# Local-attention stack on one core: pairs of 512-column instructions written as one of 1024, banks renumbered

## The chip, the cores and the metric

One NeuronCore of a Trainium2 chip (trn2) runs the whole program. The metric is the device time of one execution in microseconds, from the first to the last instruction of the core. TensorE does the matmuls and transposes; VectorE and ScalarE work between SBUF and PSUM (128 partitions, 8 banks of 512 float32 columns); GpSimd works in SBUF; SyncE issues the DMAs.

## What is computed

The input is 16 sequences of 128 tokens and 128 features. One cross-attention over a context of the same size comes first, then six layers, each of local attention (16 heads of 64, windows of 32 tokens that also see the window before) and a gated feed-forward. All of it is float32; the big products are made of three products of rounded parts.

```python
def attn_layer(x, Wqkv, qs, ksc, Wo):
    qkv = x @ Wqkv                      # 128 -> 3 * 1024
    q, k, v = jnp.split(qkv, 3, -1)     # 16 heads of 64 each
    q = l2norm(q) * qs
    k = l2norm(k) * ksc
    q = q * cos * scale + rotate_half(q) * sin * scale
    k = k * cos / scale + rotate_half(k) * sin / scale
    sim = q @ k.T * 8                   # window i against windows i - 1 and i
    attn = softmax(where(mask, -inf, sim))
    return (attn @ v) @ Wo

def ffn_layer(x, g, bln, W1, b1, W2, b2):
    xn = (x - mu) / sqrt(var + 1e-05) * g + bln
    a, gate = jnp.split(xn @ W1 + b1, 2, -1)
    return a * gelu(gate) @ W2 + b2

x = x + tanh(g_xattn) * cross_attention(layernorm(x), ctx)
h = layernorm(x)
for l in range(6):
    h = h + attn_layer(shift_tokens(h), ...)
    h = h + ffn_layer(h, ...)
out = x + tanh(g_ffn) * h
```

## The kernel before

The sequences go in pairs: 6 layers x 8 pairs are 48 pairs, and each of the pair's two items, r = 0 and r = 1, has 128 tokens on the partitions. After the cross-attention (the first 60 us) every engine runs one loop over 50 turns, in which pair `it` begins (lag 0), pair `it - 1` is in its attention (lag 1) and pair `it - 2` in its out-projection and feed-forward (lag 2). The order of the steps within a turn is written out by hand for each engine, and each engine works strictly in that order; semaphores hold it until its inputs are there. `on(lag)` says whether the pair with this lag exists.

Of one item, the work goes as follows. TensorE makes four chunks of 512 columns of q and k (`chunk`, L1199) and two of v (`v_chunk`, L1203). ScalarE squares each chunk (`square`, L623), VectorE sums the squares per head (`squares`) and multiplies the chunk by the rotation's tables (`straight`, `swapped`), GpSimd adds these (`add`) and normalises (`normalise`). TensorE transposes q and k (`turn_qk(s)`, L1207, for half s = 0 or 1 of the heads, into the two banks of `turn_qk` 2s and 2s + 1), and ScalarE copies these four banks out one by one (`heads_out(k)`, L647). ScalarE puts the mask into two score banks (`masks`), TensorE adds the scores (`scores`), VectorE takes maxima and subtracts them (`maxima(e)` L926, `minus_maxima(e)` L932, one bank e each), ScalarE takes exponentials (`exp(e)` L661), VectorE sums (`row_sums(e)` L939, then one `reciprocals`), GpSimd divides (`divide(e)` L460). TensorE transposes the probabilities (`turn_p`, L1235), ScalarE copies them (`p_out(g)` L667), TensorE multiplies by the values (`values`), ScalarE copies the output (`o_out(h)` L674). v is copied out of its banks by ScalarE (`v_out(j)` L655), and SyncE moves parts of it to other partitions by DMA (`shifted_values`).

Of a pair, the rest is: `project_out` on TensorE, `residual` on VectorE (L951), `centre` and `variance` on TensorE with `deviations` (L684) and `inverse_deviation` (L690, an Ln at L695 and an Exp at L698) on ScalarE, `normal` (L959) on VectorE, `upper_x` (L700) on ScalarE, `lower_x` (L967) on VectorE, the up-projection `up(1)`, `up(0)`, `up(2)` (L1292), `gelu` on ScalarE, `gated` (L975) on VectorE, `down` on TensorE and `feed_back` (L988) on VectorE.

Banks are shared: `BANK_USERS` lists for each bank its users in a turn, as (kind, number, r, lag), in the order of use. Before TensorE (or `masks`) writes a bank, `freed` makes it wait for the instruction that empties it of its last user (`bank_left`). Three such neighbourhoods matter below. `turn_qk(1, 1, 0)` (the transposes of half 1, lag 1, r = 0) writes the bank that `turn_qk(0, 1, 0)` had, and so waits for `heads_out(0, 1, 0)`. `v_chunk(1, 0, 0)` writes the bank of scores(1), r = 1, and waits for `minus_maxima(1, 1, 1)`. `turn_qk(0, 1, 0)` writes the bank of `v_chunk(1, 0, 0)` and waits for `v_out(1, 0, 0)`; `chunk(2, 0, 0)` follows `turn_qk(1, ...)`'s second bank of r = 1, emptied by `heads_out(1, 1, 1)`.

## Time and profile before

| | |
|---|---|
| median of 3 runs | 1455.85 us (1452.92 to 1457.2) |
| the profiled execution | 1451.59 us, span 1449.7 us |
| TensorE busy | 1357.1 us, 94% of the span |
| VectorE busy | 1294.6 us, 89% |
| ScalarE busy | 1266.6 us, 87% |
| GpSimd busy | 1184.0 us, 82% |
| matmuls / VectorE / ScalarE / GpSimd instructions | 30176 / 2400 / 2523 / 1162 |

The page's tenths over the span show the same picture from slice 4 to slice 38: all engines at 8 or 9 tenths, one turn like the other. So the reader should look at one turn with its times, and at the waits. In the page PE is TensorE, DVE VectorE, ACT ScalarE, POOL GpSimd; L12 is line 12 of the kernel. In a timeline, "x2" is two instructions of one kind in a row; their time is from the start of the first to the end of the last. Ends of matmuls are modelled.

### The profile page before, as it was taken

How to read it: one execution, taken by the hardware profiler on the slowest of the kernel's cores; microseconds unless marked ns; L12 is line 12 of the kernel's file. 1: busy time of each engine (PE TensorE's matmuls, PEld its weight loads, DVE VectorE, ACT ScalarE, POOL GpSimd, SP SyncE). 2: the span in 40 equal slices, each digit the busy share in tenths (PEclk: the TensorE clock that was granted, in tenths of full speed). 3: DMA queues.
4: the chain of work that ended last, by engine and by line, in shares of the span. 5: the costliest groups of instructions: out<-in, count | busy, mean ns of one | idle time of the engine just before them, and what ended most of it. 6: DMA issues, size and time to landing. Idle time of an engine off the chain costs nothing.

```text
span 1449.7 us, 76627 instructions
## 1 busy us (share of the span) xinstructions
PE 1357.1 (94%) x30176; PEld 1094.5 (75%) x30176; DVE 1294.6 (89%) x2400; ACT 1266.6 (87%) x2523; POOL 1184.0 (82%) x1162
## 2 busy tenths in 40 slices
PE   6589999999999999999999999999999999999985
PEld 4467777877777777777777777777777778777774
DVE  6688999999999999999999999999999999999973
ACT  6578999999999999999999999999999999899873
POOL 2687888888888888888888888888888888888860
PEclk9899999999999999999999999999999999999998
DMA  5221112131111222111122111113111112111111
GB/s 148 81 57 41 38 48 57 36 89 42 51 39 47 57 57 68 42 50 39 47 70 61 50 43 50 39 46 95 36 43 36 36 37 77 43 29 43 43 31 30
DMA packets 61752, 75.09 MB, mean 52 GB/s; under 512 B 8462, under 2 KB 35340, under 8 KB 61708
## 3 DMA queue, kind: packets, MB, share of 16 engines
q1 hardware_dynamic: 61708, 74.51, 18.8%
q8 instruction: 27, 0.44, 0.1%
q14 instruction: 17, 0.14, 0.0%
HBM read 18.90 MB, written 1.05 MB: 14 GB/s over the span
## 4 chain that ended last, share of the span: by engine, by line
PE 47%; DVE 19%; issue 15%; ACT 6%; POOL 5%; DVEq 2%; ACTq 0%; POOLq 0%
PE bank L1275 12%; PE bank L1178 6%; PE bank L1266 6%; DVE ss L906 5%; PE bank L1191 5%; PE bank L1179 4%; PE bank L1180 4%; DVE psum L943 4%; POOL u L444 3%; DVE u L913 3%; PE bank L1228 3%; PE bank L1311 3%; DVE t L922 3%; PE bank L1300 2%; ACT gate L714 2%
## 5 line engine op out<-in xcount | busy, mean ns | idle before, releaser
L444 POOL TENSOR_TENSOR u<-u,t 128x512 f32<-128x512 f32 x384 | 490.5, 1283 | 84.3 <-DVE t L922 68.5
L457 POOL TENSOR_TENSOR u<-u,rn 128x512 f32<-128x512 f32 x384 | 388.9, 1045 | 0.0
L628 ACT ACTIVATE sq<-bank 128x512 f32<-128x512 f32 x384 | 234.0, 610 | 64.0 <-PE bank L1180 62.0
L1178 PE MATMUL bank<-Wl,xsh 128*128 (+1 forms) x576 | 268.0, 465 | 15.4 <-POOL xsl L439 11.3
L463 POOL TENSOR_TENSOR P<-P,rs 128x512 f32<-128x512 f32 x192 | 196.6, 1045 | 95.0 <-DVE rs L948 95.0
L922 DVE TENSOR_TENSOR t<-bank,TS 128x512 f32<-128x512 f32 x384 | 258.7, 684 | 6.1 <-ACT sq L628 2.1
L906 DVE TENSOR_REDUCE ss<-sq 128x8 f32<-128x512 f32 x384 | 255.6, 676 | 6.4 <-issue 6.4
L913 DVE TENSOR_TENSOR u<-bank,TC 128x512 f32<-128x512 f32 x384 | 255.1, 675 | 1.3 <-ACT sq L628 1.3
L652 ACT COPY qkT<-bank 128x512 f32<-128x512 f32 x384 | 225.2, 603 | 13.5 <-PE bank L1191 6.4
L1179 PE MATMUL bank<-Wh,xsl 128*128 (+1 forms) x576 | 228.8, 397 | 0.0
L1180 PE MATMUL bank<-Wh,xsh 128*128 (+1 forms) x576 | 228.7, 397 | 0.0
L1275 PE MATMUL bank<-OT,WoS 128*128 128x256 f32 x768 | 176.7, 384 | 1.2 <-issue 1.2
L1191 PEld LDWEIGHTS bank<-shape_constants,u 64*128 64x128 f32 x3072 | 112.9, 140 | 85.4 <-issue 85.4
L1275 PEld LDWEIGHTS bank<-OT,WoS 128*128 128x128 f32 x768 | 147.9, 193 | 23.8 <-issue 1.5
L1266 PE MATMUL bank<-PT,v 64*64 64x64 f32 (+1 forms) x3072 | 154.9, 227 | 3.9 <-ACT PT L671 2.7
L1266 PEld LDWEIGHTS bank<-PT,v 64*64 64x64 f32 x3072 | 132.6, 135 | 29.2 <-issue 22.9
L1266 PE MATMUL bank<-PT,vs 64*64 64x32 f32 (+1 forms) x6144 | 153.7, 217 | 0.0
L1178 PEld LDWEIGHTS bank<-Wl,xsh 128*128 128x128 f32 x576 | 109.0, 189 | 57.7 <-issue 17.7
L1191 PE MATMUL bank<-shape_constants,u 64*128 64x64 f32 x3072 | 137.9, 230 | 14.0 <-issue 10.4
L929 DVE TENSOR_REDUCE nm<-bank 128x8 f32<-128x512 f32 x192 | 123.3, 684 | 29.6 <-PE bank L1228 29.6
L1228 PE MATMUL bank<-qkT 64*32 64x64 f32 (+1 forms) x12288 | 140.1, 220 | 8.5 <-issue 7.2
L1228 PEld LDWEIGHTS bank<-qkT 64*32 64x32 f32 x12288 | 123.7, 105 | 29.0 <-issue 27.0
(92 smaller groups left out, 2732.1 us busy)
## 6 DMA issues: line engine op xcount, KB each, us to landing
vs<-v SPq DMA_DIRECT2D x384, 128.0 KB, 2.3
Wraw<-in_L_ffn_Wqkv_dram SPq DMA_DIRECT2D x72, 117.5 KB, 2.1
WoS<-in_L_ffn_Wo_dram SPq DMA_DIRECT2D x6, 512.0 KB, 4.0
W1h<-Wh SPq DMA_DIRECT2D x6, 341.0 KB, 2.6
W1l<-Wl SPq DMA_DIRECT2D x6, 341.0 KB, 2.9
Wraw<-in_L_ffn_W_dram SPq DMA_DIRECT2D x12, 116.0 KB, 2.2
out_dram<-X SPq DMA_DIRECT2D x4, 256.0 KB, 2.7
W2S<-in_L_ffn_W_dram SPq DMA_DIRECT2D x6, 128.0 KB
```

The source lines that it names most:

```text
L444: nc.gpsimd.tensor_tensor(u[:, r, c], u[:, r, c], t2[:, r, c % 2], ALU.add).then_inc(add_done[c], 1)
L457: nc.gpsimd.tensor_tensor(by_head(u[:, r, c]), by_head(u[:, r, c]), spread(rn[:, r, HC * c:HC * c + HC], HC, DH), ALU.mult).then_inc(qk_re ...
L906: nc.vector.tensor_reduce(ss[:, r, HC * c:HC * c + HC], by_head(square_out(c, r)), AX, ALU.add).then_inc(ss_done[c], 1)
L913: nc.vector.tensor_tensor(by_head(u[:, r, c]), by_head(bank_of("chunk", c, r)[:]), TC[:, layer(it - lag), c % 2].broadcast_to([128, HC, DH ...
L922: nc.vector.tensor_tensor(halves(t2[:, r, c % 2]), halves(bank_of("chunk", c, r)[:])[:, :, ::-1, :], TS[:, layer(it - lag), c % 2].broadca ...
L1178: nc.tensor.matmul(out, x[0], Wl[:, w], start=True, stop=False)
L1179: nc.tensor.matmul(out, x[1], Wh[:, w], start=False, stop=False)
L1180: nc.tensor.matmul(out, x[0], Wh[:, w], start=False, stop=True).then_inc(done, 1)
L1191: i = nc.tensor.transpose(bank_of(kind, k + g, r)[:, at:at + 64], src[p, 128 * t:128 * t + 128], ident[p, 64 * g:64 * g + 64])
L1228: i = nc.tensor.matmul(bank_of("scores", e, r)[64 * w2 + 32 * a:64 * w2 + 32 * a + 32, at:at + (32 if w == 0 else 64)], qkT[f, r, s, 0, t, ...
L1266: i = nc.tensor.matmul(to, keys, prob, start=True, stop=True)
L1275: i = nc.tensor.matmul(bank_of("Wo")[:, 0:2 * S], WoS[:, k], OT[:, k].rearrange("p r s -> p (r s)"), start=(k == 0), stop=(k == INNER // 1 ...
```

## The change

Pairs of instructions that do the same to the two banks or halves of one item become one instruction over 1024 columns:

- VectorE: `maxima`, `minus_maxima`, `row_sums`, for both r (12 instructions a turn become 6).
- ScalarE: `exp` and `v_out` for both r, `heads_out(0)` and `heads_out(1)` for both r (`all_heads_out(0)`), `p_out(0)` and `p_out(1)` for r = 0 (`all_p_out`). `heads_out(2)`, `heads_out(3)` and the `p_out` of r = 1 stay two.
- GpSimd: `divide` for both r.

So that two banks can be one operand, the eight banks become one tensor and are renumbered; the users of each bank and their order stay. For five pairs the first bank has the higher number, and the two are then read in falling order (`[:, ::-1]`). The semaphores of the two halves become one; those of the head and probability copies get a set for each r.

The joined instruction stands where one of the two stood. `all_heads_out(0, 1, 0)` takes the place of `heads_out(0, 1, 0)`, ahead of a square; `all_heads_out(0, 1, 1)` that of `heads_out(1, 1, 1)`, ahead of `inverse_deviation`; `v_out(1, 1)` that of `v_out(0, 1, 1)`, ahead of a square and the masks of r = 1; `row_sums(1, 0)` that of `row_sums(1, 1, 0)`, behind `squares(1, 0, 0)`.

```diff
-        K = [bank(str(k)) for k in range(8)]
+        PS = es.enter_context(nc.psum_tensor("banks", [128, 8, 512], F32))
+        K = [PS[:, k] for k in range(8)]
...
+        def banks_of(kind, k=0, r=0):
+            b, b2 = (bank_place(kind, k + e, r)[0] for e in range(2))
+            return PS[:, b:b + 2] if b < b2 else PS[:, b2:b + 1][:, ::-1]
...
-                    divide(0, 2, 0)
-                    divide(1, 2, 0)
+                    divide(2, 0)
...
+                def all_heads_out(s, lag, r):
+                    pair = it - lag
+                    act.wait_ge(qk_turned[s], n_(pair * 2 + r) + 1)
+                    act.wait_ge(sc_full[s], n_(pair * 2 + r) - 1)
+                    nc.scalar.copy(qkT[:, r, s].rearrange("p w t (g i) -> p g (w t) i", g=2),
+                                   banks_of("turn_qk", 2 * s, r).rearrange("p g (k i) -> p g k i", i=64)
+                                   ).then_inc(qk_out[r][2 * s], 1)
...
                 if on(1):
-                    heads_out(0, 1, 0)
+                    all_heads_out(0, 1, 0)
                     square(1, 1, 1)
-                    heads_out(1, 1, 0)
                     heads_out(2, 1, 0)
...
-                    v_out(0, 1, 1)
+                    v_out(1, 1)
...
                     masks(0, 1, 1)
-                    v_out(1, 1, 1)
-                    exp(1, 1, 0)
-                    exp(0, 1, 0)
+                    exp(1, 0)
...
                     heads_out(3, 1, 1)
-                    heads_out(1, 1, 1)
+                    all_heads_out(0, 1, 1)
                 if on(2):
                     inverse_deviation(2)
-                if on(1):
-                    heads_out(0, 1, 1)
...
-                    p_out(1, 1, 0)
-                    p_out(0, 1, 0)
+                    all_p_out(1, 0)
...
-                    exp(0, 1, 1)
-                    exp(1, 1, 1)
+                    exp(1, 1)
                     o_out(1, 1, 0)
                 if on(0):
-                    v_out(1, 0, 0)
-                    v_out(0, 0, 0)
+                    v_out(0, 0)
...
+                def maxima(lag, r):
+                    n = (it - lag) * 2 + r
                     dve.wait_ge(scores_full[r], n_(n) + 1)
+                    nc.vector.tensor_reduce(nm[:, r], heads_of_two(banks_of("scores", 0, r)), AX, ALU.max).then_inc(mx_done, 1)
...
-                    row_sums(0, 1, 0)
                 if on(0):
                     squares(1, 0, 0)
                 if on(1):
-                    row_sums(1, 1, 0)
+                    row_sums(1, 0)
                     reciprocals(1, 0)
...
-                    maxima(0, 1, 1)
-                    maxima(1, 1, 1)
-                    minus_maxima(1, 1, 1)
-                    minus_maxima(0, 1, 1)
+                    maxima(1, 1)
+                    minus_maxima(1, 1)
```

## Rows read from the trace of the kernel before

**Rows 1.** Stretches: length, busy us of PE, PEld, DVE, ACT, POOL, clock, DMA.
```profile
662.00:944.00 282.00, 273.39 (x6243) 221.34 (x6242) 262.64 (x471) 258.63 (x511) 246.04 (x241) 1.00 0.19 51
```

**Rows 2.** Waits of whole span: who for whom, us in total, times, longest.
```profile
DVE R L956 <- PE bank L1275: 46.1, 48, 12.9
...
DVE hT L982 <- ACT gate L714: 25.3, 47, 1.7
...
PE bank L1300 <- DVE xfl L972: 18.1, 46, 1.2
...
PE bank L1191 <- issue: 10.4, 46, 0.3
```

**Rows 3.** Groups of instructions by shape: count | busy us, mean ns | idle before.
```profile
L444 POOL TENSOR_TENSOR u<-u,t 128x512 f32<-128x512 f32 x384 | 490.5, 1283 | 84.3 <-DVE t L922 68.5 <-DVE u L913 10.9
...
L628 ACT ACTIVATE sq<-bank 128x512 f32<-128x512 f32 x384 | 234.0, 610 | 64.0 <-PE bank L1180 62.0 <-DVE ss L906 1.7
...
L463 POOL TENSOR_TENSOR P<-P,rs 128x512 f32<-128x512 f32 x192 | 196.6, 1045 | 95.0 <-DVE rs L948 95.0
...
L936 DVE TENSOR_TENSOR P<-bank,nm 128x512 f32<-128x512 f32 x192 | 123.2, 684 | 1.7
...
L956 DVE TENSOR_TENSOR R<-bank,R 64x256 f32 x90 | 38.1, 423 | 31.0 <-PE bank L1275 30.4
...
L439 POOL TENSOR_TENSOR xsl<-R,xsh 128x256 fp32r<-128x256 f32 x48 | 32.8, 683 | 20.6 <-ACT xsh L621 14.3 <-issue 6.3
...
L688 ACT ACTIVATE sqx<-bank 128x256 f32<-128x256 f32 x48 | 18.2, 380 | 7.7 <-PE bank L1283 7.7
```

**Rows 4.** Timeline, ScalarE, one turn: start, us, line, operation, count [idle before].
```profile
699.98 0.60 ACT L628 ACTIVATE sq<-bank 128x512 f32<-128x512 f32 x1 [0.50 <-PE bank L1180]
...
703.84 0.42 ACT L698 ACTIVATE rstdx<-lvx 128x256 f32<-128x256 f32 x1
...
706.63 1.08 ACT L671 COPY PT<-bank 128x512 f32<-128x512 f32 x2 [0.20 <-PE bank L1191]
...
710.06 1.20 ACT L714 ACTIVATE gate<-bank,feature_columns 128x256 f32<-128x256 f32 x3
```

**Rows 5.** Timeline, VectorE, the same turn and the next one's start.
```profile
699.60 0.86 DVE L956 TENSOR_TENSOR R<-bank,R 64x256 f32 x2 [0.68 <-PE bank L1275]
...
704.66 0.49 DVE L964 SCALAR_TENSOR_TENSOR bank<-bank,feature_columns,rstdx 128x256 f32<-128x256 f32 x1
...
706.25 0.47 DVE L972 SCALAR_TENSOR_TENSOR xfl<-bank,feature_columns,xfh 128x256 fp32r<-128x256 f32 x1
...
709.74 1.29 DVE L936 TENSOR_TENSOR P<-bank,nm 128x512 f32<-128x512 f32 x2
711.54 1.27 DVE L982 SCALAR_TENSOR_TENSOR hT<-bank,feature_columns,gate 128x256 f32<-128x256 f32 x3 [0.51 <-ACT gate L714]
...
727.77 0.86 DVE L956 TENSOR_TENSOR R<-bank,R 64x256 f32 x2 [0.69 <-PE bank L1275]
```

**Rows 6.** Timeline, TensorE, the same turn.
```profile
705.88 0.71 PE L1191 MATMUL bank<-shape_constants,P 64*128 64x64 f32 x16
706.97 0.32 PE L1300 MATMUL bank<-xfh,W1l 128*85 128x256 f32 x1 [0.38 <-DVE xfl L972]
...
710.86 0.39 PE L1178 MATMUL bank<-Wl,xsh 128*128 x1
```

**Rows 7.** Timeline, all engines, 713.5 to 718.6.
```profile
714.09 1.08 ACT L659 COPY v<-bank 128x512 f32<-128x512 f32 x2
...
715.14 0.72 PE L1191 MATMUL bank<-shape_constants,u 64*128 64x64 f32 x16
...
715.34 0.97 DVE L994 SCALAR_TENSOR_TENSOR R<-bank,feature_columns,R 64x256 f32 x2
...
716.00 0.63 ACT L652 COPY qkT<-bank 128x512 f32<-128x512 f32 x1
...
716.97 0.71 PE L1191 MATMUL bank<-shape_constants,u 64*128 64x64 f32 x16 [0.22 <-issue]
```

More of the change, by code:

```diff
@@ L261, in bank_left, with when_left, both_left, item @@
                 other, ok, orr, lag = users[at]
-                before = pair + users[place][3] + turns - lag
-                if not isinstance(pair, int) or 0 <= before < PAIRS:
-                    if other in OF_PAIR:
-                        return [(s, n_(before + (LAYER_PAIRS if s is h_ready else 0)) + 1) for s in FREED[other](ok, orr)]
-                    return [(s, n_(before * 2 + orr) + 1) for s in FREED[other](ok, orr)]
-            return []
+                away = users[place][3] + turns - lag
+                if not isinstance(pair, int) or 0 <= pair + away < PAIRS:
+                    return [(s, other in COUNTS_PAIRS, orr, away) for s in FREED[other](ok, orr)]
+            return []
+        def when_left(pair, users):
+            for s, per_pair, r, away in users:
+                if per_pair:
+                    yield s, n_(pair + away + (LAYER_PAIRS if s is h_ready else 0)) + 1
+                else:
+                    yield s, n_((pair + away) * 2 + r) + 1
+        def bank_left(pair, kind, k=0, r=0):
+            return when_left(pair, user_before(pair, kind, k, r))
+        def both_left(pair, kind, k, r):
+            first, second = user_before(pair, kind, k, r), user_before(pair, kind, k + 1, r)
+            return when_left(pair, first + [user for user in second if user not in first])
         def column(at, pair, per=1, k=0, rows=slice(0, 128)):
             return fc[rows, ds(pair // LAYER_PAIRS * per + (at + k), 1)]
+        def item(t, r):
+            if len(t.shape) == 5:
+                return t[:, r].rearrange("p e g c -> p (e g) c")
+            return t[:, r].rearrange("p e g -> p (e g)")
         def layer(pair):
@@ new lines, in v_out, with exp @@
+                def v_out(lag, r):
+                    n = (it - lag) * 2 + r
+                    act.wait_ge(v_all_full[r], n_(n) + 1)
+                    act.wait_ge(pv_full, n_(n) - 1)
+                    nc.scalar.copy(v[:, r].rearrange("p (j n) -> p j n", j=2), banks_of("v", 0, r)).then_inc(v_ready, 1)
+                def exp(lag, r):
+                    n = (it - lag) * 2 + r
+                    act.wait_ge(sc_out, n_(n) + 1)
+                    ps = P[:, r].rearrange("p e g c -> p (e g c)")
+                    nc.scalar.activation(ps, ps, ACT.Exp).then_inc(exp_done, 1)
@@ L674, in o_out, with all_p_out @@
+                def all_p_out(lag, r):
+                    pair = it - lag
+                    act.wait_ge(P_turned, n_(pair * 2 + r) + 1)
+                    act.wait_ge(pv_full, n_(pair * 2 + r) - 1)
+                    nc.scalar.copy(PT[:, r].rearrange("p e (t g i) -> p g (e t) i", g=2, i=64),
+                                   banks_of("turn_p", 0, r).rearrange("p g (k i) -> p g k i", i=64)
+                                   ).then_inc(PT_ready[r][0], 1)
                 def o_out(h, lag, r):
@@ L1003, in step @@
                     straight(2, 1, 1)
-                    maxima(0, 1, 0)
-                    maxima(1, 1, 0)
-                    minus_maxima(0, 1, 0)
-                    minus_maxima(1, 1, 0)
+                    maxima(1, 0)
+                    minus_maxima(1, 0)
                 if on(0):
```

160 lines of the change are left out of this document (73 added, 87 removed).

## The prediction, made before the changed kernel was built or run

> **What bounds the kernel now.** I read the table of stretches first. In the middle of the span TensorE is busy for 273.39 of 282 us, VectorE for 262.64, ScalarE for 258.63 and GpSimd for 246.04, and the granted clock is 1.00 of its upper level, 2.4 GHz [rows 1]. So TensorE is nearest to the bound, and its idle time there is 8.6 us of 282, or 0.86 us for each turn of the loop. A turn is 28.17 us: the residual of one turn starts at 699.60, that of the next at 727.77 [rows 5]. The turns repeat almost exactly, so one of them can be walked through. No join touches a matmul. The change can therefore give back at most those 0.86 us a turn, and it takes time wherever TensorE has to wait longer.
>
> The list of waits then says where the 0.86 us lie [rows 2]: TensorE waits for the low half of the normalised features (`lower_x`, L972) 46 times, 18.1 us in all, 0.39 us each; and ahead of transposes (L1191) 46 times, 10.4 us, put down to "issue", 0.23 us each. The second has no releaser in the view, so I looked at the timeline of all engines [rows 7]. The transposes are those of `turn_qk(1,1,0)` at 716.97. They need the bank that `heads_out(0,1,0)` empties, and this copy runs 716.00 to 716.63. From ScalarE's end to TensorE's start are 0.34 us. That is the whole wait. VectorE's waits for the out-projection (46.1 us) and for the gate (25.3 us) [rows 2] show that it is paced by others.
>
> So the path that closes a turn is: end of the out-projection, residual, VectorE's and ScalarE's layernorm chain, `lower_x`, then TensorE nearly without a gap from 706.97 [rows 6] to the end of the next out-projection, with the transposes at 716.97 the one gap in which it waits for ScalarE.
>
> **What a joined instruction costs.** On ScalarE the square of 512 columns takes 610 ns and that of 256 takes 380 [rows 3]: 256 columns are 0.23 us, 512 are 0.46. A joined copy is so at most 0.61 + 0.46 = 1.07 us. Two copies one behind the other take 1.08 us in all [rows 4], as each starts before the last has quite ended. A join there saves 0.01 to 0.03 us at the end of the pair; I take 0.02. On VectorE, 512 columns of a tensor_tensor out of a bank take 684 ns and 256 take 423 (on 64 partitions, the nearest row) [rows 3], so 512 more are 0.52 us and a joined one 1.21 against 1.29 for the pair at 709.74 [rows 5]: 0.08 saved. On GpSimd a `divide` of 512 takes 1045 ns; the nearest operation in two sizes takes 1283 for 512 and 683 for 256 [rows 3], so 512 more columns would be 1.20 of 1.28 and 0.08 us are saved by a join. The two divides are between 2.09 and 2.01 us, and off the path either way. None of these rows shows 1024 columns over two banks, nor banks read in falling order, which the new layout needs for five of its pairs. I take it at the slope above; an end at nothing extra and an end at 0.1 us each bound it.
>
> Per turn VectorE loses 6 instructions, ScalarE 7, GpSimd 2. That is 6 x 0.08 = 0.5 us of VectorE and 7 x 0.02 = 0.14 us of ScalarE. Most of it lies where these engines wait for TensorE anyway (0.50 us before the square at 699.98 [rows 4], 0.68 before the residual at 699.60 [rows 5]), and is worth nothing.
>
> The rows say that ScalarE's second copy costs 0.47 us on top of the first's 0.61, and 0.46 of that are columns. The Trainium skill, "VectorE: DVE Perf Modes", section on the TRN2 errata, gives ScalarE 172 cycles plus one a column for a bank source and says that one large tile pays the fixed part once. By an estimate from that page seven joins would free 1.0 us of ScalarE a turn, and 512 more columns would cost 0.43 us and not 0.46, so that the sum below would end at 1496 and not 1498. Where instructions are back to back, the rows don't bear the larger saving out.
>
> **What it delays.** A joined instruction hands over its first half only when both are done. I went through every pair and asked who waits for the first half, and how long before that one's start it was ready.
>
> 1. *The head copies before the inverse deviation.* `heads_out(1,1,1)` stood before `inverse_deviation`, `heads_out(0,1,1)` behind it. Now both come first. Its second instruction, the Exp at 703.84, ends at 704.26 [rows 4] and comes 0.46 later: 704.72. From ScalarE's end to VectorE's start take 0.28 (the last gate ends at 711.26 [rows 4], hT starts at 711.54 [rows 5]). So `normal` starts at 705.00 and not 704.66 [rows 5]: 0.34. VectorE itself is late too: `squares(1,0,0)` now stands directly behind the residual (699.60 + 0.86 = 700.46) and its square ends at 700.58 [rows 4]; with the same hand-over it starts at 700.86, 0.40 us idle, less 0.08 for the joined sums: 704.98. The two run side by side, the later one counts. I take 0.30 (0.25 to 0.34), and `lower_x` and the up-projection at 706.97 [rows 6] move by as much.
> 2. *The score differences.* `v_chunk(1,0,0)` at 710.86 [rows 6] needs the bank of scores(1,1,1). `minus_maxima(1)` came first of its pair and was done at 709.74 + 0.68 = 710.42; VectorE to TensorE takes 0.25 (`lower_x` ends at 706.72 [rows 5], TensorE starts at 706.97 [rows 6]), so the bank was ready 0.19 before it was wanted. Joined, it is ready 0.52 later, less 0.08 for the joined maxima. 0.52 - 0.08 - 0.19 = 0.25. VectorE and TensorE both carry delay 1, which cancels.
> 3. *The first head copy of r = 0.* `turn_qk(1,1,0)` waits for `heads_out(0,1,0)`, now `all_heads_out`, 0.46 longer. Its start can be 0.10 nearer to its transposes: they end at 715.86 and the copy starts at 716.00 [rows 7], while elsewhere it takes 0.04 (706.59 [rows 6] to 706.63 [rows 4]). 0.46 - 0.10 = 0.36. TensorE already waits here, so all of it shows. Behind it TensorE has `turn_p`, the last v chunks, values, scores and `chunk(3,0,0)`; ScalarE's next copies need these transposes, so its chain to `x_parts` and the xsl moves along, and nothing catches up.
>
> Other joins hold back a first half and hide it. `v_out(0,0)` gives its first bank at 715.1 + 0.34, where `turn_qk(0,1,0)` stands at 715.14 [rows 7]; but delays 1 and 2 have moved that to 715.7, so it is covered as long as they are there, and costs 0.3 if they are not. The joined `all_heads_out(0,1,1)` frees chunk(2,0,0)'s bank 0.46 later, which eats TensorE's idle time before the up-projection, not more. The joined exp and sums of r = 1 make the reciprocals 0.5 late; `divide` and `turn_p` follow them with under 0.4 us to spare after delay 3. The joined v copies of r = 1 bring exp(1,0) forward by 0.3, to no one's use. SP's shifted values waited for the second v copy before as well. The bank numbers alone cost nothing; they name the same sequence of users.
>
> **The sum.** 0.30 + 0.25 + 0.36 = 0.91 us a turn. The three occur in 46, 47 and 47 turns: 13.8 + 11.8 + 16.9 = 42.5 us. The profiled execution took 1451.59 us (span 1449.7), so its successor would take 1494; the median of the runs is 4.3 us above the profiled one, which gives 1498.
>
> **The rivals.** *Hidden in part*: one or two of the delays are covered by slack I misjudge. Delays 1 and 2 rest on 0.2 us of slack each; delay 3 alone gives 17 us, 1473, and two of them 1482. For it: hand-over times are read from one place each. *Faster*: TensorE's wait at 716.97 is not for the copy but for something else ahead of it in the same queues (`feed_back`, which ends at 716.31 [rows 7], is the other one in question), and the chain to `lower_x` has the slack. Then ScalarE and VectorE reach their points 0.1 to 0.2 us earlier a turn, 0.2 x 46 = 9 us, 1447. It decides where the fixed part of an instruction is above 0.2 us; the pairs show under 0.1, and the end-to-start 0.34 of ScalarE recurs, so I give it little. The Trainium skill's fixed costs ("VectorE: DVE Perf Modes", the same section) would point this way. *No effect*: joins split again or all within slack, 1456. *More*: reading over two banks costs 0.1 us extra each and falls on three delays and the v copies, 0.3 to 0.4 us a turn more, 1515.
>
> **Chances.** Forecast 0.60 (own range 1484 to 1506); hidden in part 0.17; more 0.07; faster 0.10; no effect 0.06. Differences under 0.3% (4 us) can't be told from none. So faster 0.10, same 0.06, slower 0.84. The range takes the first two and half of "more": 1462 to 1514.
>
> **What the profile of the changed kernel would show.** A turn of 29.1 us; TensorE's busy share in the middle down from 97% to 94%; its wait before `turn_qk(1,1,0)` at about 0.6 us; a new wait of 0.25 us before `v_chunk(1,0,0)` released by VectorE's P; joined copies of 1.05 us on ScalarE and 1.21 on VectorE. Joined ones under 0.9 us would make me wrong, as would turns in which `turn_qk(1,1,0)` doesn't follow the end of the joined copy by 0.34 us.

## The result, and the profile after

The changed kernel takes 1485.01 us, the median of 4 runs (1481.63 to 1487.11), beside 1454.38 us for the kernel before in 4 runs (1448.48 to 1457.2). The ratio is 1.0214, with a 95% interval of 1.0175 to 1.0252: slower by 30.6 us, where the forecast was slower by 42.5. The profiled execution of the changed kernel took 1481.63 us, with a span of 1479.8.

The page's first part: busy time of each engine, its share of the span, instructions.

```profile
PE 1374.1 (93%) x30176; PEld 1100.9 (74%) x30176; DVE 1286.0 (87%) x2112; ACT 1244.8 (84%) x2187; POOL 1171.9 (79%) x1066
```

Every engine but TensorE has less to do than before (VectorE 1294.6, ScalarE 1266.6, GpSimd 1184.0), and the kernel is slower all the same. The middle of the span, as in [rows 1]:

```profile
662.00:944.00 282.00, 270.43 (x5992) 217.31 (x5986) 253.77 (x400) 247.89 (x432) 237.59 (x216) 1.00 0.18 50
```

TensorE is idle for 11.6 us of 282 and not 8.6. A turn is 28.92 us, so that is 1.19 us a turn and not 0.86. This is less than half of what a turn has grown by. The rest, 0.42 us a turn, is counted as busy, 27.73 us and not 27.31 for the same matmuls: a product is recorded at 0.39 to 0.40 us while the one behind it can start 0.23 after it, so the first 0.17 us or so of a wait behind a product disappears in its modelled end. So I take waits from starts and not from idle time. The granted clock is 1.00 here as before. The waits of the whole span, as in [rows 2] (us in total, times, longest):

```profile
DVE banks L991 <- ACT rstdx L734: 22.3, 48, 3.2
...
PE banks L1211 <- ACT qkT L679: 21.3, 46, 0.5
PE banks L1320 <- DVE xfl L999: 20.8, 47, 1.2
...
DVE psum L971 <- ACT P L693: 12.7, 47, 0.5
```

The wait before `turn_qk(1,1,0)`, 10.4 us in [rows 2] and put down to "issue", is now 21.3 us and names the joined head copy. The forecast's new wait ahead of `v_chunk(1,0,0)` isn't in this list; its 0.18 us are among those that count as busy, and show in the starts of TensorE's rows below. The joined instructions by shape (count, busy us, mean ns, idle before), as in [rows 3]:

```profile
L486 POOL TENSOR_TENSOR P<-P,rs 128x1024 f32<-128x1024 f32 x96 | 183.0, 1906 | 111.6 <-DVE rs L976 111.6
...
L963 DVE TENSOR_TENSOR P<-banks,nm 128x1024 f32<-128x1024 f32 x96 | 117.6, 1225 | 7.3
...
L693 ACT ACTIVATE P<-P 128x1024 f32<-128x1024 f32 x96 | 101.8, 1061 | 4.0 <-DVE P L963 3.4
L679 ACT COPY qkT<-banks 128x1024 f32<-128x1024 f32 x96 | 98.9, 1030 | 11.4 <-PE banks L1211 11.3
L687 ACT COPY v<-banks 128x1024 f32<-128x1024 f32 x96 | 96.5, 1006 | 0.2 <-PE banks L1200 0.2
```

One turn on ScalarE, as in [rows 4] (start, us, line, operation):

```profile
712.23 1.04 ACT L679 COPY qkT<-banks 128x1024 f32<-128x1024 f32 x1
713.14 0.51 ACT L731 ACTIVATE lvx<-banks,cols 128x256 f32<-128x256 f32 x1
713.68 0.42 ACT L734 ACTIVATE rstdx<-lvx 128x256 f32<-128x256 f32 x1
...
723.83 1.02 ACT L687 COPY v<-banks 128x1024 f32<-128x1024 f32 x1
...
726.02 1.01 ACT L679 COPY qkT<-banks 128x1024 f32<-128x1024 f32 x1 [0.20 <-PE banks L1211]
```

The same turn on VectorE, as in [rows 5], from one residual to the next. The two residuals bound the turn that the table below takes apart:

```profile
709.09 0.86 DVE L983 TENSOR_TENSOR R<-banks,R 64x256 f32 x2 [0.59 <-PE banks L1295]
710.10 0.69 DVE L934 TENSOR_REDUCE ss<-sq 128x8 f32<-128x512 f32 x1 [0.16 <-ACT sq L649]
...
714.49 0.49 DVE L991 SCALAR_TENSOR_TENSOR banks<-banks,feature_columns,rstdx 128x256 f32<-128x256 f32 x1 [0.38 <-ACT rstdx L734]
...
719.51 1.23 DVE L963 TENSOR_TENSOR P<-banks,nm 128x1024 f32<-128x1024 f32 x1
...
738.00 0.86 DVE L983 TENSOR_TENSOR R<-banks,R 64x256 f32 x2 [0.60 <-PE banks L1295]
```

And on TensorE, as in [rows 6] and [rows 7]: the up-projection, `v_chunk(1,0,0)`, `turn_qk(0,1,0)`, `turn_qk(1,1,0)`.

```profile
716.81 0.32 PE L1320 MATMUL banks<-xfh,W1l 128*85 128x256 f32 x1 [0.42 <-DVE xfl L999]
...
720.57 0.28 PE L1322 MATMUL banks<-xfh,W1h 128*128 128x256 f32 x1
720.88 0.50 PE L1198 MATMUL banks<-Wl,xsh 128*128 x1
...
725.20 0.71 PE L1211 MATMUL banks<-shape_constants,u 64*128 64x64 f32 x16
...
727.27 0.71 PE L1211 MATMUL banks<-shape_constants,u 64*128 64x64 f32 x16 [0.46 <-ACT qkT L679]
```

`v_chunk(1,0,0)` starts 0.31 us after the matmul ahead of it. In the kernel before it was 0.12, and that matmul's row is not among the rows ahead:

```profile
710.74 0.29 PE L1302 MATMUL bank<-xfh,W1h 128*128 128x256 f32 x1
```

With these starts a turn can be cut into parts, and the parts of two kernels compared. The parts are, each from start to start: residual to up-projection (A), up-projection to `v_chunk(1,0,0)` (B), from there to `turn_qk(0,1,0)` (C), to `turn_qk(1,1,0)` (D), and to the next residual (E). All in us, read from the same timelines of each kernel near 700 us; where two turns in a row differ, both values stand. The last column is a turn near there; it is within 0.03 us of the median over all the turns of that profile.

| kernel | A | B | C | D | E | turn |
|---|---|---|---|---|---|---|
| before | 7.37 | 3.90 | 4.29 | 1.83 | 10.80 | 28.17 |
| after | 7.72 | 4.08 | 4.32 | 2.07 | 10.72 | 28.92 |
| all joined (control) | 7.72 | 4.07 | 4.27 | 2.19 | 10.74, 10.82 | 29.05 |
| banks only | 7.37 | 3.89 | 4.28 | 1.83 | 10.75, 10.81 | 28.15 |
| heads of r = 0 apart | 7.72 | 4.07 | 4.27 | 1.81 | 10.77, 10.85 | 28.65 |
| heads of r = 1 apart | 7.37 | 4.08 | 4.29 | 2.19 | 10.73, 10.83 | 28.70 |
| scores of r = 1 apart | 7.72 | 3.89 | 4.39 | 2.19 | 10.74, 10.83 | 28.97 |
| scores 1 and v 0 apart | 7.72 | 3.89 | 4.26 | 2.20 | 10.75, 10.84 | 28.84 |
| three apart | 7.37 | 3.88 | 4.40 | 1.76 | 10.78, 10.89 | 28.24 |
| four apart | 7.38 | 3.88 | 4.26 | 1.78 | 10.91, 10.99 | 28.24 |
| sums first | 7.72 | 4.08 | 4.26 | 2.19, 2.24 | 10.73, 10.84 | 29.07 |
| before, waits turned | 7.37 | 3.90 | 4.29 | 1.59 | 10.93, 10.96 | 28.05 |
| after, waits turned | 7.72 | 4.07 | 4.27 | 1.99 | 10.72 | 28.79 |
| six apart, waits turned | 7.37 | 3.89 | 4.29 | 1.59 | 10.85, 10.95 | 28.03 |

After against before, a turn grows by 0.35 + 0.18 + 0.03 + 0.24 - 0.08 = 0.72 us in this turn, and by 0.73 between the medians of the 47 turns (28.18 and 28.91). From the first residual to the last the profiles take 1327.1 and 1360.0 us: 32.9 more. Ahead of the first residual the changed kernel's profiled execution is 2.8 us shorter (101.8 against 104.6), with a granted clock of 0.91 against 0.87 from 60 to 100 us. Outside the loop differences of some us come and go between executions with the granted clock there (0.74 in the profile of `e3_heads1_apart`, from 60 to 100 us), so below I read turns first and medians second. The experiments were run in three sets, each with runs of the kernel before beside it (medians 1453.99, 1452.85 and 1455.10 us), so two experiments are compared by their ratios and not by their times.

### The profile page after: what moved, and what is told of

Its sections match the earlier page's. It is cut to its first block, busy times and chain, and to the rows that moved or that the text cites. A ratio compares the mean times of both kernels' runs of the same rounds, so it can differ in the third digit from the quotient of the medians.

```text
span 1479.8 us, 75430 instructions
## 1 busy us (share of the span) xinstructions
PE 1374.1 (93%) x30176; PEld 1100.9 (74%) x30176; DVE 1286.0 (87%) x2112; ACT 1244.8 (84%) x2187; POOL 1171.9 (79%) x1066
## 3 DMA queue, kind: packets, MB, share of 16 engines
HBM read 18.90 MB, written 1.05 MB: 13 GB/s over the span
## 4 chain that ended last, share of the span: by engine, by line
PE 56%; DVE 15%; issue 12%; ACT 8%; POOL 3%; DVEq 1%; ACTq 0%; POOLq 0%
PE banks L1295 11%; PE banks L1286 8%; PE banks L1198 7%; PE banks L1199 5%; PE banks L1200 5%; PE banks L1211 5%; DVE u L941 4%; PE banks L1331 4%; DVE psum L971 4%; PE banks L1320 3%; DVE ss L934 3%; ACT sq L649 3%; PE banks L1248 3%; PE banks L1321 2%; PE banks L1322 2%
## 5 line engine op out<-in xcount | busy, mean ns | idle before, releaser
L649 ACT ACTIVATE sq<-banks 128x512 f32<-128x512 f32 x384 | 231.3, 603 | 84.8 <-PE banks L1200 83.4
L1198 PE MATMUL banks<-Wl,xsh 128*128 (+1 forms) x576 | 280.5, 487 | 17.8 <-POOL xsl L462 11.6
L486 POOL TENSOR_TENSOR P<-P,rs 128x1024 f32<-128x1024 f32 x96 | 183.0, 1906 | 111.6 <-DVE rs L976 111.6
L950 DVE TENSOR_TENSOR t<-banks,TS 128x512 f32<-128x512 f32 x384 | 258.4, 683 | 4.8 <-ACT sq L649 1.6
L941 DVE TENSOR_TENSOR u<-banks,TC 128x512 f32<-128x512 f32 x384 | 254.7, 674 | 1.8 <-ACT sq L649 1.8
L1199 PE MATMUL banks<-Wh,xsl 128*128 (+1 forms) x576 | 228.8, 397 | 0.0
L1200 PE MATMUL banks<-Wh,xsh 128*128 (+1 forms) x576 | 228.3, 396 | 0.0
L1295 PE MATMUL banks<-OT,WoS 128*128 128x256 f32 x768 | 175.5, 382 | 1.2 <-issue 1.2
L1211 PE MATMUL banks<-shape_constants,u 64*128 64x64 f32 x3072 | 137.9, 229 | 26.5 <-ACT qkT L679 21.3
L1286 PE MATMUL banks<-PT,v 64*64 64x64 f32 (+1 forms) x3072 | 155.3, 228 | 2.7 <-ACT PT L706 1.4
L1286 PE MATMUL banks<-PT,vs 64*64 64x32 f32 (+1 forms) x6144 | 154.0, 217 | 0.0
```

The lines of the kernel that those rows point to most:

```text
L649: nc.scalar.activation(square_out(c, r), bank_of("chunk", c, r)[:], ACT.Square).then_inc(sq_done[c], 1)
L941: nc.vector.tensor_tensor(by_head(u[:, r, c]), by_head(bank_of("chunk", c, r)[:]), TC[:, layer(it - lag), c % 2].broadcast_to([128, HC, DH ...
L1198: nc.tensor.matmul(out, x[0], Wl[:, w], start=True, stop=False)
L1199: nc.tensor.matmul(out, x[1], Wh[:, w], start=False, stop=False)
L1200: nc.tensor.matmul(out, x[0], Wh[:, w], start=False, stop=True).then_inc(done, 1)
L1211: i = nc.tensor.transpose(bank_of(kind, k + g, r)[:, at:at + 64], src[p, 128 * t:128 * t + 128], ident[p, 64 * g:64 * g + 64])
```

## The experiments

Theory: each of the three delays of the forecast comes from one join that makes TensorE wait, and undoing that join takes that delay alone away. Rivals: joined instructions over two banks are slow in themselves; the path over VectorE's sums sets `normal`; the layout of the banks matters.

All kernels below compute everything. Most of them come from one form of the changed kernel in which any join can be undone by a switch. Where a diff below shows instructions, it shows what the switch makes of them. For this form, each half and each r has a semaphore of its own, counted by pairs:

```diff
-        mx_done, sc_out, sum_done, rs_done = (sem(s) for s in ("mx_done", "sc_out", "sum_done", "rs_done"))
+        mx_done, sc_out, sum_done, exp_done, P_ready, v_ready = (
+            [sems(name + str(r), 2) for r in range(2)] for name in ("mx_done", "sc_out", "sum_done", "exp_done", "P_ready", "v_ready"))
+        rs_done = sem("rs_done")
```

**All joined, in this form (`e0_all_joined`).** The control: nothing else is changed against the changed kernel. It was run after the next eight, whose expectations therefore start from the changed kernel's 28.92 us a turn and not from the control's 29.05.

> Control for the runs before: all joins of the changed kernel, with the semaphores of the experiments (one for each half and r, counted by pairs). In the changed kernel TensorE starts 0.24 us after the end of the joined head copy, in the experiments 0.36 to 0.39. TensorE's queue tells why, I think: there the wait for the copy stands in front of the register instruction that works out the next wait's value, together with that for the normalised heads. My theory: hand-over 0.38, a turn of 29.07 us, ratio 1.026 to 1.030, and e7 (29.08) is no slower than its control. Rival (e7's order of sums costs 0.16 itself): 28.92 us.

Ratio to before 1.0271 (1.0241 to 1.0301), 1494.27 us. A turn is 29.05 us and not 28.92, and the difference lies in D, 2.19 against 2.07; C is 0.05 shorter, and E longer by about as much. ScalarE and TensorE there:

```profile
699.71 1.02 ACT L698 COPY qkT<-banks 128x1024 f32<-128x1024 f32 x1 [0.16 <-PE banks L1297]
```

```profile
701.08 0.71 PE L1297 MATMUL banks<-shape_constants,u 64*128 64x64 f32 x16 [0.58 <-ACT qkT L698]
```

The copy ends at 700.73 and the transposes start 0.35 later. In the changed kernel they follow their copy by 727.27 - 727.03 = 0.24. The copy and the transposes are the same, only the bookkeeping of semaphores differs. So this control is what the experiments are compared with, and the 0.11 are a question of their own (the last three experiments).

**The banks alone (`e1_banks_only`).** New numbers and one tensor, every join undone:

```diff
-                    all_heads_out(0, 1, 0)
+                    heads_out(0, 1, 0)
                     square(1, 1, 1)
+                    heads_out(1, 1, 0)
...
-                    maxima(1, 1)
-                    minus_maxima(1, 1)
+                    maxima(0, 1, 1)
+                    maxima(1, 1, 1)
+                    minus_maxima(1, 1, 1)
+                    minus_maxima(0, 1, 1)
```

> The eight banks as one tensor and renumbered, every instruction in its two parts and in the order of the kernel before. My theory (three waits on a first half cost the time): ratio 1.000 to the kernel before, a turn of 28.17 us. Rival (the layout itself costs, through other banks being neighbours): a good part of the 2.1%, a turn of 28.4 us or more.

Ratio 0.9998 (0.998 to 1.0017), 1453.65 us; a turn of 28.15. The layout costs nothing that can be told from none, and the loss is in the joins. That the joined instructions cost nothing extra for two banks or for a falling order is in the rows of the changed kernel: 1006 to 1061 ns on ScalarE, where the slope of [rows 3] gives at most 1070, and 1225 on VectorE, where it gives 1210. The head copy of r = 0 reads its banks in falling order and takes 1.01 us, that of r = 1 in rising order and takes 1.04.

**The head copies of r = 0 apart (`e2_heads0_apart`).**

```diff
-                    all_heads_out(0, 1, 0)
+                    heads_out(0, 1, 0)
                     square(1, 1, 1)
+                    heads_out(1, 1, 0)
```

> The changed kernel with the head copy of r = 0 in two again, at the old places. My theory: the transposes turn_qk(1,1,0) wait for half a copy, the 0.24 us between the two transposes come back, 46 times: 11 us less than the changed kernel, 1474 us, ratio 1.0135. The size that I forecast (0.36) would give 17 us less. Rival (joined instructions are slow of themselves or load a shared port): 1 or 2 us, as one of twelve joins is gone.

Ratio 1.0149 (1.0109 to 1.0189), 1476.13 us. A turn is 28.65, 0.40 under the control (0.37 by the medians of all turns); D falls from 2.19 to 1.81, and nothing else moves by more than 0.01. This is delay 3, alone, at the control's hand-over. The expectation had 0.24, the changed kernel's size.

**The head copies of r = 1 apart (`e3_heads1_apart`).**

```diff
-                    all_heads_out(0, 1, 1)
+                    heads_out(1, 1, 1)
                 if on(2):
                     inverse_deviation(2)
+                if on(1):
+                    heads_out(0, 1, 1)
```

> The changed kernel with the head copy of r = 1 in two again, the second half behind the inverse deviation. My theory: the Exp of the inverse deviation ends 0.35 us sooner, normal and lower_x follow: up to 0.35 us a turn, 16 us less, 1469 us, ratio 1.010. If the joined sums behind squares(1,0,0) hold VectorE too, as I wrote beforehand, only about 0.05 us come back and the ratio stays at 1.020.

Ratio 1.0156 (1.0118 to 1.0193), 1476.96 us. A turn is 28.70, 0.35 under the control, all of it in A (7.72 to 7.37). This is delay 1, alone. This join delays a second thing, the bank of `chunk(2,0,0)`, which starts 4.33 us after the residual in the changed kernel and 4.11 in the kernel before. That isn't what sets A: TensorE still has 0.42 us idle before the up-projection, and waits there for `lower_x`.

**The score maxima and differences of r = 1 apart (`e4_scores1_apart`).**

```diff
-                    maxima(1, 1)
-                    minus_maxima(1, 1)
+                    maxima(0, 1, 1)
+                    maxima(1, 1, 1)
+                    minus_maxima(1, 1, 1)
+                    minus_maxima(0, 1, 1)
```

> The changed kernel with maxima and differences of r = 1 in two again. v_chunk(1,0,0) then starts 0.18 us sooner in the turn. Each delay by itself: 8 us less, ratio 1.016. My theory with the cover I named: the joined v copy of r = 0 ends 0.35 us before turn_qk(0,1,0) starts and holds it, so that TensorE loses there what it gained: within 2 us of the changed kernel, ratio 1.020.

Ratio 1.027 (1.0232 to 1.0307), 1493.54 us: no gain that the times show against the control's 1494.27. The turns say why. B falls from 4.07 to 3.89, so delay 2 is 0.18 and it is gone, but C rises from 4.27 to 4.39. ScalarE's and TensorE's rows there:

```profile
705.21 1.02 ACT L712 COPY v<-banks 128x1024 f32<-128x1024 f32 x1
```

```profile
705.36 0.57 PE L1284 MATMUL banks<-Wl,xsh 128*128 x1
706.46 0.71 PE L1297 MATMUL banks<-shape_constants,u 64*128 64x64 f32 x16
```

The joined v copy ends at 706.23, and `turn_qk(0,1,0)`, which needs its bank, starts at 706.46, 1.10 after the product ahead of it. Without a wait it is 0.97 (below). The v copy is ready to take the place of delay 2. C takes back 0.12 of the 0.18; the 0.06 that should be left are 3 us, and the medians don't show them.

**The same with the v copies of r = 0 apart (`e9_scores1_v0_apart`).** To test that reading:

```diff
-                    v_out(0, 0)
+                    v_half_out(1, 0, 0)
+                    v_half_out(0, 0, 0)
```

> The changed kernel with two joins in two again: scores of r = 1 and v copy of r = 0. The scores alone gave nothing back (28.96 against 28.92 us a turn), which I put down to the v copy: it would hold turn_qk(0,1,0) as soon as TensorE gets there sooner. If so, both together give 0.15 to 0.2 us: 28.75 us a turn. If the scores' join costs nothing at all: 28.9.

Ratio 1.0253 (1.0225 to 1.028), 1486.72 us. A turn is 28.84, 0.13 under the last one and 0.21 under the control. The interval overlaps those of the last experiment and of the control, so the times alone don't tell these three apart; their turns do. C is back at 4.26:

```profile
698.59 1.08 ACT L706 COPY v<-banks 128x512 f32<-128x512 f32 x2
```

```profile
698.74 0.57 PE L1284 MATMUL banks<-Wl,xsh 128*128 x1
699.71 0.72 PE L1297 MATMUL banks<-shape_constants,u 64*128 64x64 f32 x16
```

The product is now followed by the transposes after 0.97, with the copies starting at the same place of the turn (0.15 ahead of that product in both kernels). The v copy was the cover.

**The row sums ahead of the squares' sums (`e7_sums_first`).** The rival for delay 1: VectorE itself is late at `normal` because `squares(1,0,0)` stands directly behind the residual and waits.

```diff
+                if on(1):
+                    row_sums(1, 0)
                 if on(0):
                     squares(1, 0, 0)
                 if on(1):
-                    row_sums(1, 0)
                     reciprocals(1, 0)
```

> The changed kernel with the joined sums of r = 0 ahead of squares(1,0,0) and not behind it. This tells what delays normal: VectorE's own queue (0.16 us idle before squares(1,0,0)) or the Exp on ScalarE. By the profile of the changed kernel normal waits 0.38 us for the Exp, so the order on VectorE is worth nothing: a turn of 28.92 us, ratio 1.021. If it were VectorE's queue: 28.8 us.

Ratio 1.0304 (1.0281 to 1.0328), 1496.77 us; a turn of 29.07 beside 29.05. VectorE's row for `normal`:

```profile
722.71 0.49 DVE L1066 SCALAR_TENSOR_TENSOR banks<-banks,feature_columns,rstdx 128x256 f32<-128x256 f32 x1 [0.63 <-ACT rstdx L765]
```

VectorE now has 0.63 us to spare ahead of it, where it had 0.38 in the changed kernel, and `normal` still starts 5.41 us after the residual (5.40 in the changed kernel). ScalarE's Exp sets it, and not VectorE.

**Three apart (`e5_three_apart`).** The edits of `e2_heads0_apart`, `e3_heads1_apart` and `e4_scores1_apart` together. In the common form each group of joins is a pair of switches, for r = 0 and r = 1:

```diff
-HEADS = [True, True]
+HEADS = [False, False]
...
-SCORES = [True, True]
+SCORES = [True, False]
```

> The changed kernel with the three named joins in two again: head copies of r = 0 and r = 1, scores of r = 1. If nothing but them cost time, the turn is that of the kernel before, 28.17 us, or less. By the cover I named, the joined v copy of r = 0 now holds turn_qk(0,1,0) by about 0.2 us and the head copy behind it by 0.1 to 0.15: a turn of 28.3 us, ratio 1.004.

Ratio 1.0046 (1.0029 to 1.0063), 1459.93 us. A turn is 28.24, 0.81 under the control. Three joins make nearly the whole loss; 0.07 a turn is left, with C at 4.40 held by the v copy as above.

**Four apart (`e6_four_apart`).** The v copies of r = 0 apart as well, as in `e9_scores1_v0_apart`:

```diff
-VS = [True, True]
+VS = [False, True]
```

> As the last, and the v copy of r = 0 in two as well. The joins that are left (maxima and differences of r = 0, both sums, both exponentials, v copy of r = 1, probability copy of r = 0, both divides) have no one waiting for a first half. My theory: a turn of 28.10 to 28.17 us, ratio 0.996 to 1.001. Rival (joined instructions cost of themselves): at least half of the 0.75 us a turn is still there, 28.5 us.

Ratio 1.0017 (1.0002 to 1.0031), 1455.94 us, and yet the turn is 28.24 again. C falls to 4.26 as it should, and E rises by as much, from 10.78 to 10.91. TensorE and GpSimd at `turn_qk(1,1,0)` and `turn_p`:

```profile
690.55 0.72 PE L1297 MATMUL banks<-shape_constants,u 64*128 64x64 f32 x16 [0.18 <-issue]
691.16 0.71 PE L1297 MATMUL banks<-shape_constants,P 64*128 64x64 f32 x16
```

```profile
688.91 1.91 POOL L500 TENSOR_TENSOR P<-P,rs 128x1024 f32<-128x1024 f32 x1 [1.37 <-DVE rs L1051]
```

The divide ends at 690.82, and `turn_p` starts 0.34 later, 0.61 after `turn_qk`; where the divide is early, it starts 0.52 after it. So 0.09 of the 0.13 are the chain of exp, sums, reciprocals and divide, the next limit. The other 0.04 weren't traced. The expectation of 28.10 to 28.17 us was missed for this reason.

**The kernel before, its two waits turned (`e13_before_waits_turned`).** Now for the 0.11 us by which the changed kernel's hand-over beats that of its own control. The traces hold the instructions of TensorE's queue too, which are not counted as busy (`PEldq`; line, operation, ns, start). Ahead of `turn_qk(1,1,0)` the kernel before has an instruction that waits for the head copy, a register instruction that waits for the normalised heads, and one that waits for `feed_back` and adds to a counter:

```profile
L1173 PEldq EVENT_SEMAPHORE  x1: 51/51/51, 716.7 to 716.7; - x1
L1173 PEldq ALU_OP  x1: 32/32/32, 716.8 to 716.8; - x1
L1186 PEldq EVENT_SEMAPHORE  x1: 51/51/51, 716.9 to 716.9; - x1
```

In the changed kernel the register instruction is the one that waits for the copy, and only the last one stands behind it:

```profile
L1205 PEldq ALU_OP  x1: 32/32/32, 727.1 to 727.1; - x1
L1206 PEldq EVENT_SEMAPHORE  x1: 51/51/51, 727.2 to 727.2; - x1
```

With the trace's finer times, the copy of the kernel before ends at 716.63, the three start at 716.66, 716.77 and 716.86, the first weights load at 716.94 and the first transpose starts at 716.97. In the changed kernel the copy ends at 727.03, the two start at 727.07 and 727.16, the weights at 727.24, the transpose at 727.27. The control has three again, as the kernel before. In the built program the count that the changed kernel's wait for the copy needs is worked out just ahead of it, by a register instruction that waits for the heads; in the control the v copies are counted by pairs too, so that this count is there already, and the wait for the copy comes first again.

The wait for the copy is the one that is met last. Theory: what stands behind it in the queue is worked off after the copy's end, and so is paid every turn. Put it last, and the hand-over is shorter. Rival: 0.34 us is a fixed time from ScalarE to TensorE, and the 0.24 has another cause. The edit is the order of two lines in `turn`, and so for all transposes:

```diff
-                    freed(lag, kind, k, r)
                     freed(lag, kind, k + 1, r)
+                    freed(lag, kind, k, r)
```

> The kernel before, with one edit: ahead of transposes TensorE waits for the second bank's last user first and for the first bank's last user last, so that the wait for the head copy stands on the transpose itself and the register work for the other wait is done before. No join. If register work behind a wait is part of the hand-over, the 0.34 us from the copy to turn_qk(1,1,0) fall by 0.10 to 0.15: a turn of 28.03 us, ratio 0.996. If the hand-over is the semaphore's own time: no change, 28.17.

Ratio 0.9958 (0.9943 to 0.9973), 1448.78 us: faster than the kernel before by 0.4%. The wait for the copy now stands in the last instruction of the queue, together with that for `feed_back`. This instruction, ScalarE, TensorE and GpSimd:

```profile
L1186 PEldq EVENT_SEMAPHORE  x1: 325/325/325, 686.6 to 686.6; - x1
```

```profile
686.27 0.63 ACT L652 COPY qkT<-bank 128x512 f32<-128x512 f32 x1
```

```profile
687.00 0.71 PE L1191 MATMUL bank<-shape_constants,u 64*128 64x64 f32 x16
687.60 0.72 PE L1191 MATMUL bank<-shape_constants,P 64*128 64x64 f32 x16
```

```profile
685.22 2.05 POOL L463 TENSOR_TENSOR P<-P,rs 128x512 f32<-128x512 f32 x2 [1.09 <-DVE rs L948]
```

The copy ends at 686.90, the waiting instruction at 686.94, and TensorE starts at 687.00: 0.10 and not 0.34, so D is 0.24 shorter, and A, B and C are as before. E gives 0.13 to 0.16 back, of which, as in `e6_four_apart`, the divide explains a part: the divides end at 687.27, and `turn_p` starts 0.33 later and 0.60 after `turn_qk`, not 0.52. So the 0.34 is no fixed time from ScalarE to TensorE. 0.12 us a turn are left, times 47 makes 5.6, and the medians differ by 6.3.

**The changed kernel, its two waits turned (`e14_after_waits_turned`).**

```diff
-            return when_left(pair, first + [user for user in second if user not in first])
+            return when_left(pair, second + [user for user in first if user not in second])
```

> The changed kernel with the same edit. Its hand-over is 0.24 us; with the wait on the transpose itself 0.05 to 0.10 less: a turn of 28.84 us, ratio 1.018. If the hand-over has nothing to do with register work: 28.92, ratio 1.021.

Ratio 1.016 (1.013 to 1.019), 1480.14 us. The last instruction of the queue now waits for the copy, and alone:

```profile
L1206 PEldq EVENT_SEMAPHORE  x1: 51/51/51, 731.9 to 731.9; - x1
```

The hand-over is 0.15 us where it was 0.24; the turn goes from 28.92 to 28.79. The interval overlaps that of the changed kernel (1.0175 to 1.0252), so here too it is the turns that tell. The same lever works in both kernels. C falls from 4.32 to 4.27 as well.

**Six apart and the waits turned (`e15_six_apart_waits_turned`).** What is left of the change when every join that was found to hold TensorE is undone, the exponentials and sums of r = 1 among them, so that its divide is early:

```diff
-VS = [True, True]
-EXPS = [True, True]
+VS = [False, True]
+EXPS = [True, False]
...
-SUMS = [True, True]
+SUMS = [True, False]
```

with the three edits of `e5_three_apart` and that of `e14_after_waits_turned`.

> The joins that no one waits on, with the turned waits: maxima and differences, exponentials and sums of r = 0 joined, v copy of r = 1, probability copy of r = 0, divides; the head copies, the scores, exponentials and sums of r = 1 and the v copy of r = 0 in two. In e6 turn_p waited 0.08 us for the divided P of r = 1; with exponentials and sums in two it shouldn't. My theory: as e13, 28.0 us a turn, ratio 0.995; joins are worth nothing beyond it. If joins that hold back no one gave time to the path: below 27.9 us.

Ratio 0.995 (0.9934 to 0.9966), 1449.51 us; turns of 27.98 and 28.07. It is ahead of both kernels, but not of `e13_before_waits_turned`: the joins that are left (v of r = 1, exponential, sums and scores of r = 0, the probabilities, both divides) are worth nothing that the times show. The gain is the order of two waits. `turn_p` starts 0.55 us after `turn_qk` here, so its divide no longer holds it by much, and E is still 10.85 to 10.95: what E gives back is only in part the divide.

## Why the prediction was right, and where its sizes were off

**Sign and place: right, and shown.** The loss is in the loop, at a clock of 1.00 before and after, and undoing three joins takes 0.81 of the control's 0.88 us a turn away (0.80 of 0.84 by the medians of all turns). The forecast's three delays are the three changes in A, B and D, and each is undone by its own join and no other. The times agree: by the ratios `e2_heads0_apart` is 17.7 us under the control and `e3_heads1_apart` 16.7, where 0.40 x 47 and 0.35 x 47 give 18.8 and 16.5.

**Delay 1, forecast 0.30, measured 0.35.** That these are near each other is in part luck: two errors nearly cancel. I took 0.28 from ScalarE's end to VectorE's start, from the gate. The same rows held the value of this very place: the Exp ends at 704.26 [rows 4], `normal` starts at 704.66 [rows 5], 0.40; after, it is 714.10 to 714.49, 0.39. The 0.40 is made of three instructions of VectorE's queue between the two, one of which waits for the Exp. With it the delay would have been 0.46. But the Exp came 0.35 later and not 0.46. ScalarE's two rows of before, not among the rows ahead:

```profile
702.27 1.08 ACT L652 COPY qkT<-bank 128x512 f32<-128x512 f32 x2
703.33 0.48 ACT L695 ACTIVATE lvx<-bank,cols 128x256 f32<-128x256 f32 x1
```

The Ln started 0.02 us before the copies' end; behind the joined copy it starts 0.13 before that (713.14 against 713.27). So 0.11 of slack lay there. The trace's queue records say what it was: ahead of the Ln, ScalarE waits for the variance, and this wait was met only at 703.22, 0.11 before the Ln started. In the changed kernel it is met at 712.71, long before the joined copy ends. VectorE's own path, which I gave the same weight, doesn't count: the square's hand-over there is 0.03 (710.07 to 710.10), its idle time 0.16 and not 0.40, and `e7_sums_first` shows no effect.

**Delay 2, forecast 0.25, measured 0.18.** The mechanism is that of the forecast. The size went wrong at VectorE's hand-over to TensorE: I took 0.25, as from `lower_x`. The joined differences end at 720.74 and `v_chunk(1,0,0)` starts at 720.88: 0.14. So the old bank, given up at 710.42 [rows 5] for a start at 710.86 [rows 6], had been ready 0.30 and not 0.19 before it was wanted. The joined differences take 1.23 us and the first of the two took 0.68, 0.55 more; they start 10.42 us after the residual and not 10.14, 0.28 later under a delay 1 of 0.35, so the joined maxima save 0.07. 0.55 - 0.07 - 0.30 = 0.18.

**Delay 3, forecast 0.36, measured 0.24.** This is the term of the sum that was most off, 0.12 x 47 = 5.6 us of the 12 between the forecast and the medians. The copy is 1.01 us instead of the 0.63 that the single one took here [rows 7], 0.38 longer and not 0.46. Its start is 0.03 nearer to the transposes (0.11 against 0.14), not 0.10. And the hand-over is 0.24 and not 0.34. 0.38 - 0.03 - 0.10 is 0.25, the 0.24 of part D. The last is no property of the join: in the control it is 0.35 and D grows by 0.36, as forecast. The change also counts the semaphores of the head copies anew, for each r, and by that one instruction fewer stands in TensorE's queue behind the wait for the copy. I had costed this part at nothing.

**The covers.** The forecast said that the joined v copy would cost 0.3 at `turn_qk(0,1,0)` once delays 1 and 2 are gone. It costs 0.12 to 0.14 (4.39 and 4.40 against 4.26), so the cover is right, but it is delay 2 alone: C is 4.39 with delay 1 and 4.40 without it. The 0.03 by which C is longer in the changed kernel are not the v copy: with the same joins C is 4.27 in the control and in `e14_after_waits_turned`. The other named one, divide and `turn_p` with under 0.4 us to spare, shows up in `e6_four_apart` and `e13_before_waits_turned`, when delay 3 or the hand-over is taken away. Part E is 0.08 shorter in the changed kernel. It holds the same wait for GpSimd's `xsl` as before (0.24 and 0.25 us). The time shows first at the probability copies of r = 1, which are not joined: they start 1.32 us after `turn_qk(1,1,0)` and not 1.39. Why stays open.

**The sum.** Per turn 0.91 forecast, 0.73 measured, 32.9 us over the loop and 30.1 in the profiles' spans, since the head of that execution was 2.8 us shorter. Of the 9.6 us between 42.5 and 32.9, delay 3 is 5.6, delay 2 is 3.3 and part E 3.8, while delay 1 and part C take 2.3 and 1.4 back. TensorE's share in the middle is 95.9%, not the 94% forecast, as over half of the new waiting is counted as busy. For the same reason the 0.86 us of idle time were no strict ceiling on what a turn can give back. The wait before `turn_qk(1,1,0)` is 0.46, not 0.6; the joined copies 1.01 to 1.04, where 1.05 stood. `turn_qk(1,1,0)` doesn't follow its copy by 0.34, which the forecast named as a sign of being wrong, and it was: that number was the weakest of the sum.

**The rivals.** *Hidden in part* is wrong as a whole, since all three delays are there, but its reason was at work in small: slack that I misjudged took 0.11 us each from delays 1 and 2, and two hand-over times read from one place each were wrong for another. *Faster* is refuted: TensorE's wait is for the copy, as `e2_heads0_apart` and `e13_before_waits_turned` show, and less work on ScalarE and VectorE was worth nothing. *More*, at 0.1 us extra for two banks, is refuted by the shapes. *No effect* is what `e1_banks_only` is, not the change.

**What a join saves.** By the busy times of the spans, ScalarE has 21.8 us less, 0.46 a turn over 47 turns and 0.07 for each of its seven joins; VectorE 8.6, 0.03 for each of six; GpSimd 12.1, 0.13 for each of two. I had taken 0.02, 0.08 and 0.08. Where two stood back to back the rows give VectorE more, 0.06 us (1.28 to 1.22 for the maxima, 1.29 to 1.23 for the differences). The Trainium skill, "VectorE: DVE Perf Modes", TRN2 errata, from which I worked out 1.0 us a turn for ScalarE, gives about twice what the rows do. Either way it is time in which these engines would have waited.

## What to carry to other kernels

A joined instruction gives its first half away as late as its second, so before joining, ask for each half who waits for it and how long it had been ready: 0 to 0.3 us of slack against 0.4 to 0.55 us of delay decided this change, and the saving of 0.03 to 0.13 us an instruction fell on engines that were waiting anyway. A busy share with modelled ends hides short waits, so compare starts. When one delay is taken away, look for the next one a tenth of a microsecond behind it; three of the repairs here were eaten in part that way. And where an engine waits for several semaphores ahead of one instruction, write the wait that is met last as the last, and look at how its queue was built: that gave 0.4% here, and the joins nothing.

## What the runs showed of the hardware that was not expected

The time from the end of a ScalarE copy to the start of the TensorE transposes that wait for it is no constant; it is set by what stands in TensorE's queue behind the wait. In each of these kernels, over 41 or 42 turns, the waiting instruction is recorded, or ends, 0.04 us after the copy's end. Each queue instruction behind it starts 0.09 to 0.11 us after the one ahead (up to 0.15 in some turns), the weights load 0.08 us after the start of the last one, and the transpose starts 0.03 later. With two instructions behind the wait (the kernel before and the control) that makes 0.34 to 0.39, with one (the changed kernel) 0.24 to 0.28. With none it is 0.15 where the last instruction waits for the copy alone (`e14_after_waits_turned`) and 0.10 where it waits for the copy and for a semaphore met earlier (`e13_before_waits_turned` and `e15_six_apart_waits_turned` alike); where those 0.05 come from stays open. That the work behind the wait is what costs is in these times, and was tested by moving the wait. VectorE's hand-over to TensorE differs in the same way in the changed kernel: ahead of `v_chunk(1,0,0)` it is 0.14 us with no instruction behind the waiting one, which is recorded at 720.78, and ahead of the up-projection (716.56 to 716.81) it is 0.25 with one behind the waiting one (716.60 and 716.70). These two are read from one turn, and no wait was moved there.

Reading two banks with one instruction, in falling order of their numbers too, costs nothing beyond the columns on ScalarE (1006 and 1030 ns against 1070 by the slope), and at most 15 ns on VectorE (1225 against 1210), where all the joined pairs stand in falling order. GpSimd's divide over 1024 columns takes 1.91 us where two of 512 took 2.05 to 2.09: the fixed part of this operation is some 0.14 to 0.18 us, more than the two sizes of its neighbour in [rows 3] showed.
